# A cross-attention and feed-forward kernel: the scale parameters loaded behind the first token tile, and the hand-written order of five engines rewritten

## The chip, the cores and the metric

One core of one Trainium2 chip runs the kernel. The time is the device time of one execution in microseconds (us), the median over runs. "Words" of 4 bytes are float32; a "tile" of tokens is 128 tokens of 2048 features.

## The reference

Two stages on x of shape (2, 1024, 2048), both with a residual sum:

```python
def fake_quant(x, scale, zp):
    q = jnp.clip(jnp.round(x / scale + zp), 0, 255)
    return (q - zp) * scale
x = x + fake_quant(layernorm(x), s1, z1) @ fake_quant(ctx, s2, z2)   # ctx (2, 2048, 2048)
u = layernorm(x)
probs = softmax(u @ W_router.T); top 2 of 8 experts, renormalised -> w
base = u @ W_base.T + b_base                                          # W_base (2048, 2048)
lora = einsum('ter,eor,te->to', einsum('td,erd->ter', u, lora_A), lora_B, w) * 2.0
x = x + base + lora                                                   # 8 experts of rank 16
```

Both scales are 8/255, both zero points 128. The four numbers arrive as a small input (`qp`), so the kernel reads them at run time.

## The kernel before

Everything is one program for one core, with explicit semaphores. `XA`, `EX`, `Q`, `S` are the large buffers on the chip, `PS` the 8 banks in which TensorE sums, `par`, `cst`, `rr`, `flag`, `WC`, `mv`, `st` small ones.

**The first matmul.** For each of the 16 token tiles: `xn_load` (L375) brings it in two halves, `ln1_stats` (L573, L578) makes mean and variance on VectorE, `ln1_coef` (L583 to L593) makes scale and offset from them and from the parameters in five small steps on GpSimd, `ln1_quant` (L607) quantises to one byte on ScalarE or VectorE, `ln1_turn` (L625) transposes on TensorE, `ln1_back` (L635, L637) brings the result back as bf16. Between the first transposes stand filler matmuls (`warm`, L650), whose result nobody reads. The 32 slices `g` of ctx (16 for each batch) come by `ctx_load` (L380), are quantised by `ctx_quant` (L662 on ScalarE) and turned into bf16 by `ctx_conv` (L672, L674). `gemm1` (L694) multiplies them, a half of 512 tokens and 8 of 16 blocks of the sum at a time, and `evac1` (L706, L709) adds x. `keep` stores the sum to the output in DRAM.

**The second normalisation.** Of batch 0 the sums over features are made along the way: `add0`, `square0`, `sqadd0` add up on GpSimd and ScalarE, `offset_total` (L826) and `var_total` (L839) turn the sums into one number a token by one-column matmuls against `mean_w`, 8 for the offsets and 8 for the variances. `y_scale`, `y_high`, `y_diff1` to `y_diff4` and `y_low` (L1031) make seven operands out of the normalised tokens, each as a float16 value and a float16 remainder. Those of batch 1 are made later, go to DRAM (`yd_store`, 64 pieces) and come back by seven `y_load`s of 2048 KB, one for each operand, when batch 0 is done with the buffers.

**The second matmul.** `lora_h` (L1087 to L1089) gives lora_A times the tokens, `route` (L1163) the router's logits. Then 16 pairs `i` of row blocks of W_base, 8 for each batch, each as seven products (`product`, L1470 to L1472, 24 matmuls each, by which four quarters of a pair come from seven multiplications instead of eight), with tails for the experts (`tail`, L1483 to L1485), `post` (L1526, L1532) for scale and bias, and `store` (L537), by which GpSimd has a DMA add the result onto the output in DRAM. The weights of pair `i` come by `raw_load` in two halves; `w_squares` (L1325), `w_norm` (L1338), `w_total` (L882, one matmul of one column), `w_root` (L886) and `w_factors` make a scale from them, `w_scale` (L1377), `w_add` (L1402, L1406, L1415), `w_high` (L1422) and `w_low` (L1428) their float16 operands.

**What sets the order.** Each engine has its own list of calls, written out by hand: `sync_program`, `tensor_program`, `scalar_program`, `vector_program`, `pool_program`, some 1,900 calls in all. An engine works strictly through its list; each call first waits for its semaphores. Which engine does a call, and the count at which a semaphore stands for it, come from tables (`BACK`, `CTXQ`, `YLO`, `WLO`, `POST`, `WSC`, `KEEP`, `GEMM`, `EVAC`, `WHI`, `PROD`), which have to follow the order of the lists. Ahead of the lists `sync_first`, `vector_first` and `pool_first` run. Then every engine asks in `case_of` (L1999 to L2001) which case the parameters make:

```python
eng.wait_ge(*par_ok["flag"])
return eng.value_load(flag[0:1, 0:1], min_val=0, max_val=2)
```

`params` (L554 to L565) has VectorE make eight small values out of `par`, the last of them `flag` (0 where both zero points are 128). A flag above 0 sends the engines through `general_...` first, which these inputs do not need.

## Time and profile before

| | before |
|---|---|
| median of 3 runs (lowest, highest) | 960.43 us (956.87, 961.31) |
| the profiled execution, its span | 960.41 us, 958.6 us |
| mean granted clock of TensorE, share of full speed | 0.996 |
| TensorE busy, matmul | 931.6 us, 97% |
| TensorE busy, weight load (beside it) | 443.1 us, 46% |
| VectorE, ScalarE, GpSimd busy | 585.5, 506.9, 310.2 us |
| instructions | 13081 |
| read from DRAM, written to it | 137.44 MB, 56.62 MB |

The span runs from the first to the last instruction of the core; the time of the execution has 1.8 us more. A busy time says how long an engine had work under way, not that it was held up by nothing: a matmul at half the clock counts as busy. The loss at half the clock is therefore to be had only from the granted clock of single stretches. PE in the rows is TensorE, DVE VectorE, ACT ScalarE, POOL GpSimd, SP SyncE; a "q" behind the name is that engine's DMA issue. In the column of waits, "a <- b" says that the instruction of line a began when the one of line b was done.

### The profile page before, as it was taken

The page shows a single profiled execution, that of the slowest core. Times are in us where ns is not written, and L with a number is a line of the kernel's source. Part 1 is how long each engine was busy: PE and PEld are TensorE (multiplying, and loading weights), DVE is VectorE, ACT ScalarE, POOL GpSimd, SP SyncE. Part 2 cuts the span into 40 slices and gives each one's busy share as a digit, 9 for nine tenths or more (in the row PEclk, how much of TensorE's full clock was granted, in tenths as well). Part 3 has the DMA queues.
Part 4 walks back from the last instruction along what each step waited for, and adds up shares of the span by engine and source line. Part 5 has one row for each costly group of instructions (what it writes and reads, how often), then busy time and mean ns, then how long its engine had stood idle before and what let it go on. Part 6 is the DMA issues. An engine that isn't in the chain of part 4 may idle for free. (4 is left out here: it accounts for less than half of the span.)

```text
span 958.6 us, 13081 instructions
## 1 busy us (share of the span) xinstructions
PE 931.6 (97%) x4594; PEld 443.1 (46%) x4614; DVE 585.5 (61%) x729; ACT 506.9 (53%) x495; POOL 310.2 (32%) x249
## 2 busy tenths in 40 slices
PE   4899999999999999999999999999999999999998
PEld 3754445444444443444444444444444444444443
DVE  6886877899787846566877977326432524425421
ACT  4866894668864737465575665334422322342320
POOL 4574985273532253261212212150210202111200
PEclk9999999999999999999999999999999999999999
DMA  9999698879835676657678767987314223342331
GB/s 345 412 412 393 219 376 298 299 255 307 293 67 181 198 243 209 221 146 242 200 211 276 181 223 188 345 308 214 117 22 116 50 93 72 98 123 75 85 66 44
DMA packets 61445, 197.08 MB, mean 206 GB/s; under 512 B 5696, under 2 KB 22208, under 8 KB 52928
## 3 DMA queue, kind: packets, MB, share of 16 engines
q1 hardware_dynamic: 55904, 176.26, 50.9%
q0 software_dynamic: 5472, 19.93, 12.6%
q8 instruction: 41, 0.67, 0.3%
q14 instruction: 28, 0.23, 0.1%
HBM read 137.44 MB, written 56.62 MB: 202 GB/s over the span
## 5 line engine op out<-in xcount | busy, mean ns | idle before, releaser
L1470 PE MATMUL PS<-XA,Q 128*128 128x512 f16 x384 | 145.6, 379 | 0.0
L1472 PE MATMUL PS<-XA,Q 128*128 128x512 f16 x384 | 145.5, 379 | 0.0
L1471 PE MATMUL PS<-XA,Q 128*128 128x512 f16 x384 | 145.5, 379 | 0.0
L1428 POOL TENSOR_TENSOR S<-S 128x1024 f16<-128x1024 f32 x29 | 64.6, 2233 | 169.4 <-ACT S L1422 169.4
L694 PE MATMUL PS<-Q,S 128*128 128x512 bf16 x501 | 112.7, 383 | 2.2 <-DVE S L709 1.3
L694 PE MATMUL PS<-EX,S 128*128 128x512 bf16 (+1 forms) x535 | 105.7, 354 | 3.5 <-POOL S L674 1.6
L1422 ACT ACTIVATE Q<-S 128x1024 f16<-128x1024 f32 x64 | 66.6, 1050 | 73.2 <-PE PS L1472 29.5
L1470 PE MATMUL PS<-EX,S 128*128 128x512 f16 x256 | 97.0, 379 | 0.5 <-ACT Q L1532 0.5
L1471 PE MATMUL PS<-EX,S 128*128 128x512 f16 x256 | 97.0, 379 | 0.0
L1472 PE MATMUL PS<-EX,S 128*128 128x512 f16 x256 | 97.0, 379 | 0.0
L1377 ACT ACTIVATE S<-S,WC 128x1024 f32<-128x1024 f32 x64 | 70.7, 1137 | 46.1 <-DMA S<-in_wT_dram 31.4
L1422 ACT ACTIVATE S<-S 128x1024 f16<-128x1024 f32 x48 | 49.6, 1051 | 78.1 <-DVE S L1406 26.1
L1428 DVE TENSOR_TENSOR Q<-S,Q 128x1024 f16<-128x1024 f32 x52 | 64.2, 1244 | 40.5 <-ACT Q L1422 40.5
L1526 DVE SCALAR_TENSOR_TENSOR Q<-PS,WC,Q 128x512 f32<-128x512 f32 x36 | 26.8, 748 | 92.6 <-PE PS L1485 75.8
L694 PEld LDWEIGHTS PS<-Q,S 128*128 128x128 bf16 x512 | 50.3, 99 | 64.3 <-issue 4.4
L694 PEld LDWEIGHTS PS<-EX,S 128*128 128x128 bf16 x544 | 53.0, 98 | 52.4 <-issue 2.4
L662 ACT ACTIVATE S<-S,cst 128x2048 uint8<-128x2048 f32 x28 | 58.2, 2086 | 19.2 <-DMA S<-in_cT_dram 19.0
L537 POOL DMA_DIRECT2D out_dram<-Q x30 | 26.5, 941 | 124.1 <-DVE Q L1534 64.9
L1470 PEld LDWEIGHTS PS<-XA,Q 128*128 128x128 f16 x384 | 37.6, 98 | 45.7 <-issue 1.1
L1472 PEld LDWEIGHTS PS<-XA,Q 128*128 128x128 f16 x384 | 37.6, 98 | 45.3
L1471 PEld LDWEIGHTS PS<-XA,Q 128*128 128x128 f16 x384 | 37.6, 98 | 45.0 <-issue 0.3
L1428 POOL TENSOR_TENSOR Q<-S,Q 128x1024 f16<-128x1024 f32 x12 | 28.6, 2386 | 90.4 <-ACT Q L1422 90.4
(244 smaller groups left out, 1722.7 us busy)
## 6 DMA issues: line engine op xcount, KB each, us to landing
S<-in_cT_dram SPq DMA_DIRECT2D x32, 1024.0 KB, 7.7
S<-in_wT_dram SPq DMA_DIRECT2D x32, 1024.0 KB, 6.1
out_dram<-Q POOLq DMA_DIRECT2D x30, 512.0 KB, 5.6
EX<-in_xn_dram SPq DMA_DIRECT2D x24, 512.0 KB, 7.7
yops_dram<-S SPq DMA_DIRECT2D x48, 256.0 KB, 3.4
XA<-in_xT_dram SPq DMA_DIRECT2D x16, 512.0 KB, 7.9
out_dram<-XA SPq DMA_DIRECT2D x16, 512.0 KB, 7.6
out_dram<-S SPq DMA_DIRECT2D x16, 512.0 KB, 4.3
```

The costliest lines, as they stand in the source:

```text
L537: e.dma_start(outT[b, o], ob[(2 * i + h) % 3], accum_op=ALU.add).then_inc(stored.of(2 * i + h), 16)
L662: e.activation(u8b[g % 2], ctx_f[g % 2], ACT.Identity, bias=z2, scale=inv2).then_inc(ctxq.of(g), 1)
L694: last = e.matmul(bank(a)[:, t0 % 512:t0 % 512 + t1 - t0], q2[q][:, 128 * k:128 * (k + 1)], q1T[b][:, k, t0:t1], start=(k == 0), stop=(k = ...
L1377: e.activation(v, v, ACT.Copy, bias=0.0, scale=w_cols(i)[:, 4:5]).then_inc(w_scaled.of(i, q), 1)
L1422: e.activation(ring[slot_of(i, n)][:, 0:1024], W_SRC[n], ACT.Copy, bias=0.0, scale=1.0).then_inc(w_hi.of(i, n), 1)
L1428: e.tensor_tensor(v[:, 1024:2048], W_SRC[n], v[:, 0:1024], ALU.subtract).then_inc(w_lo.of(i, n), 1)
L1470: e.matmul(bank(bk), wh, yh(op, k), start=(fresh and k == 0), stop=False, skip_group_check=not fresh)
L1471: e.matmul(bank(bk), wh, yl(op, k), start=False, stop=False, skip_group_check=not fresh)
L1472: last = e.matmul(bank(bk), wl, yh(op, k), start=False, stop=(read and k == 7), skip_group_check=not fresh)
L1526: e.scalar_tensor_tensor(dst, src, kk, dst, op0=ALU.mult, op1=ALU.add).then_inc(post_ok.of(i, n), 1)
```

## The change

`load_par` goes from the head of SyncE's list to behind the first token tile's `xn_load`, and VectorE makes the first tile's statistics ahead of `params`. The lists of all five engines are rewritten. No call changes its engine and none is added or removed; the tables are reordered to follow. Two lines of them and the pieces of the lists of which the text speaks:

```diff
@@ -49,68 +49,68 @@
     ('sq', 1), ('sq', 3)]}
...
     def sync_first(e):
-        load_par(e); xn_load(e, 0, 0); xn_load(e, 0, 1); xn_load(e, 0, 2); ctx_load(e, 0); xn_load(e, 0, 3); ctx_load(e, 1)
+        xn_load(e, 0, 0); load_par(e); xn_load(e, 0, 1); xn_load(e, 0, 2); ctx_load(e, 0); xn_load(e, 0, 3); ctx_load(e, 1)
...
-        x_load(e, 17, general); keep(e, 12); keep(e, 16); ctx_load(e, 21); load_bias(e); ctx_load(e, 20)
...
-        x_load(e, 24, general); b_load(e, 0); keep(e, 23); ctx_load(e, 28); x_load(e, 25, general); keep(e, 24)
...
+        x_load(e, 24, general); ctx_load(e, 28); keep(e, 23); x_load(e, 25, general); keep(e, 24); ctx_load(e, 29)
...
-        ln_load(e, 7); yd_store(e, 7, 0); yd_store(e, 7, 4); raw_load(e, 8, 1); yd_store(e, 7, 3); yd_store(e, 7, 2)
-        yd_store(e, 7, 6); yd_store(e, 7, 1); yd_store(e, 7, 7); yd_store(e, 7, 5); a_reload(e); b_load(e, 8); y_load(e, 0)
-        raw_load(e, 8, 0); y_load(e, 1); y_load(e, 2); y_load(e, 3); y_load(e, 5); y_load(e, 4); raw_load(e, 9, 1)
...
+        keep(e, 30); keep(e, 31); tile_load(e, 0); tile_load(e, 1); load_bias(e); raw_load(e, 1, 1); b_load(e, 1)
...
+        yd_store(e, 6, 6); ln_load(e, 7); raw_load(e, 8, 1); a_reload(e); yd_store(e, 7, 3); yd_store(e, 7, 2)
+        yd_store(e, 7, 6); yd_store(e, 7, 1); yd_store(e, 7, 5); yd_store(e, 7, 0); yd_store(e, 7, 7); yd_store(e, 7, 4)
+        raw_load(e, 8, 0); y_load(e, 0); y_load(e, 1); y_load(e, 2); y_load(e, 3); y_load(e, 5); y_load(e, 4); b_load(e, 8)
...
     def tensor_program(e):
...
-        gemm1(e, 18, 0, 512, 0, 8); gemm1(e, 18, 512, 1024, 0, 8); offset_total(e, 0); offset_total(e, 1)
-        var_total(e, 0, 0); var_total(e, 0, 1); gemm1(e, 18, 0, 512, 8, 16); gemm1(e, 18, 512, 1024, 8, 16)
...
+        r_total(e); gemm1(e, 17, 0, 512, 8, 16); offset_total(e, 0); offset_total(e, 1); gemm1(e, 18, 0, 512, 0, 8)
+        gemm1(e, 18, 0, 512, 8, 16); var_total(e, 0, 0); gemm1(e, 19, 512, 1024, 0, 8); var_total(e, 0, 1)
...
-        gemm1(e, 31, 0, 512, 8, 16); lora_h(e, 0, [0]); w_total(e, 0); lora_h(e, 0, [1]); lora_h(e, 0, [2])
-        lora_h(e, 0, [3]); lora_h(e, 0, [4]); lora_h(e, 0, [5]); lora_h(e, 0, [6]); lora_h(e, 0, [7])
...
+        gemm1(e, 31, 512, 1024, 8, 16); lora_h(e, 0, [0]); w_total(e, 0); lora_h(e, 0, [1]); lora_h(e, 0, [2])
+        lora_h(e, 0, [3]); lora_h(e, 0, [4]); lora_h(e, 0, [5]); lora_h(e, 0, [6]); clear(e, 0); lora_h(e, 0, [7])
-        product(e, 0, 0, 4, 5); clear(e, 0); product(e, 0, 0, 5, 6); product(e, 0, 0, 6, 7); product(e, 0, 0, 7, 8)
...
-        product(e, 1, 2); product(e, 1, 3); product(e, 1, 4); tail(e, 1, 2); w_total(e, 2); product(e, 1, 5)
...
+        product(e, 1, 3); product(e, 1, 4); w_total(e, 2); tail(e, 1, 2); product(e, 1, 5); product(e, 1, 6); tail(e, 1, 0)
...
-        ctx_quant(e, 19); square0(e, 14); square0(e, 15); ctx_quant(e, 18); add1_first(e); ctx_conv(e, 18); ctx_quant(e, 20)
...
-        copy(e, 7); y_high(e, 1, 7, "B"); y_high(e, 1, 7, "A"); y_high(e, 1, 7, "T"); y_high(e, 1, 7, "4"); w_scale(e, 8, 3)
-        w_high(e, 7, 5); post(e, 7, 2); a_high(e, 1, 0); a_high(e, 1, 1); w_scale(e, 8, 2); w_scale(e, 8, 0)
...
+        ctx_quant(e, 19); ctx_quant(e, 18); square0(e, 15); ctx_conv(e, 18); add1_first(e); ctx_quant(e, 21)
...
+        w_high(e, 7, 4); post(e, 6, 6); y_high(e, 1, 7, "T"); w_high(e, 7, 5); y_high(e, 1, 7, "4"); b_high(e, 7)
+        post(e, 7, 2); w_scale(e, 8, 3); w_scale(e, 8, 2); a_high(e, 1, 0); a_high(e, 1, 1); w_high(e, 8, 1); post(e, 7, 3)
...
     def vector_first(e):
-        params(e)
+        ln1_stats(e, 0, 0); params(e)
...
-        w_low(e, 1, 5); store(e, 0, 0); w_low(e, 1, 6); sqadd1(e, 6); sqadd1(e, 8); w_root(e, 2); store(e, 0, 1)
-        w_low(e, 2, 2); store(e, 1, 0); w_low(e, 2, 6); sqadd1(e, 9); w_low(e, 2, 5); sqadd1(e, 10); w_root(e, 3)
...
+        sqsum1_move(e, 1); sqadd1(e, 2); sqsum1_move(e, 3); w_low(e, 1, 2); sqadd1(e, 4); store(e, 0, 0); store(e, 0, 1)
+        w_low(e, 1, 5); w_low(e, 1, 6); sqadd1(e, 6); sqadd1(e, 8); w_root(e, 2); w_low(e, 2, 2); store(e, 1, 0)
```

The instructions of SyncE's queue at the start, before (`in_qp` holds the parameters, `in_xn` the token tiles, `in_cT` the slices of ctx; the first two tiles lie in `EX`):

```order
L362 DMA par<-in_qp_dram 128x4
L375 DMA EX<-in_xn_dram 128x1024 x4
L375 DMA XA<-in_xn_dram 128x1024 x2
L380 DMA S<-in_cT_dram 128x2048
L375 DMA XA<-in_xn_dram 128x1024 x2
```

And now:

```order
L375 DMA EX<-in_xn_dram 128x1024 x2
L362 DMA par<-in_qp_dram 128x4
L375 DMA EX<-in_xn_dram 128x1024 x2
L375 DMA XA<-in_xn_dram 128x1024 x2
L380 DMA S<-in_cT_dram 128x2048
```

The parameters have moved behind the two halves of the first tile. On VectorE the first tile's statistics (L573, L578) have moved ahead of the small values (L556 and on), in the same way:

```order
 L2028 UNCONDITIONAL_BRANCH
+L573 BN_STATS st<-EX 128x6 x4
+L578 BN_AGGR mv<-st 128x2
 L556 RECIPROCAL cst<-par 128x1
 L557 RECIPROCAL cst<-par 128x1
```

TensorE in the first matmul, where the sums of batch 0 become one number a token (L826 the offsets, L839 the variances, L694 the first matmul, about 165 us into the program):

```order
+L694 MATMUL PS<-Q,S 128x512 x8
 L826 MATMUL PS<-mean_w,S 128x1 x8
-L839 MATMUL PS<-mean_w,S 128x1 x8
-L694 MATMUL PS<-Q,S 128x512 x80
+L694 MATMUL PS<-Q,S 128x512 x16
+L839 MATMUL PS<-mean_w,S 128x1 x4
+L694 MATMUL PS<-Q,S 128x512 x8
+L839 MATMUL PS<-mean_w,S 128x1 x4
+L694 MATMUL PS<-Q,S 128x512 x72
```

The variances' eight one-column matmuls stood right behind the offsets'; now 16 matmuls of `gemm1` stand between, and 8 more between the halves.

GpSimd around the first stores of the second matmul (L537 `store`, L1428 `w_low`, L819 `sqadd1`, L886 `w_root` of pair 2):

```order
+L1428 TENSOR_TENSOR Q<-S,Q 128x1024
 L819 TENSOR_TENSOR S<-S 128x1024
-L1428 TENSOR_TENSOR Q<-S,Q 128x1024
-L1428 TENSOR_TENSOR S<-S 128x1024
-L537 DMA out_dram<-Q 128x1024
-L1428 TENSOR_TENSOR S<-S 128x1024
+L537 DMA out_dram<-Q 128x1024 x2
+L1428 TENSOR_TENSOR S<-S 128x1024 x2
 L819 TENSOR_TENSOR S<-S 128x1024 x2
 L886 TENSOR_TENSOR WC<-WC,cst 128x1
```

The first store has moved ahead of one `w_low`, and the second from behind `w_root` to right behind the first.

## Rows read from the trace of the kernel before

**Rows 1.** Of the page, part 1: busy us and share of the span, instructions.
```profile
PE 931.6 (97%) x4594; PEld 443.1 (46%) x4614; DVE 585.5 (61%) x729; ACT 506.9 (53%) x495; POOL 310.2 (32%) x249
```

**Rows 2.** Waits of TensorE: what, line <- releaser: us, times, longest us.
```profile
PE PS L625 <- ACT S L607: 13.6, 2, 12.3
PE PS L882 <- DVE WC L1338: 2.1, 1, 2.1
...
PE PS L694 <- DVE S L709: 1.3, 2, 1.1
PE PS L1087 <- DVE XA L1031: 1.0, 1, 1.0
PE PS L1470 <- ACT Q L1532: 0.5, 1, 0.5
...
PE PS L694 <- ACT S L672: 0.3, 1, 0.3
```

**Rows 3.** Busy by stretch: us, PE, PEld, DVE, ACT, POOL; PEclk, DMA, GB/s.
```profile
165.00:167.70 2.70, 2.62 (x23) 2.47 (x24) 2.70 (x4) 0.33 (x1) 0.00 (x0) 1.00 0.97 252
167.70:171.20 3.50, 3.50 (x10) 1.29 (x9) 2.66 (x5) 3.50 (x2) 0.00 (x0) 0.51 1.03 419
365.70:369.20 3.50, 3.50 (x10) 1.20 (x9) 2.58 (x7) 2.57 (x3) 1.31 (x2) 0.51 0.53 60
```

**Rows 4.** Timeline of SyncE's queue at the start: start us, us, what.
```profile
0.74 0.39 SPq L362 DMA_DIRECT2D par<-in_qp_dram  x1
1.18 1.84 SPq L375 DMA_DIRECT2D EX<-in_xn_dram  x4
```

**Rows 5.** DMA issues: KB each, us from issue to landing.
```profile
Braw<-in_rT_dram SPq DMA_DIRECT2D x1, 64.0 KB, 9.5
par<-in_qp_dram SPq DMA_DIRECT2D x1, 2.0 KB, 1.6
```

**Rows 6.** Timeline of VectorE from 2.4 us.
```profile
2.40 0.16 DVE L556 RECIPROCAL cst<-par 128x1 f32<-128x1 f32 x1 [2.40 <-DMA par<-in_qp_dram]
3.09 0.16 DVE L565 TENSOR_TENSOR flag<-rr 128x1 int32<-128x1 f32 x1
5.50 2.56 DVE L573 BATCH_NORM_STATS2 st<-EX 128x6 f32<-128x512 f32 x4 [2.25 <-DMA EX<-in_xn_dram]
8.10 0.26 DVE L578 BATCH_NORM_AGGREGATE mv<-st 128x2 f32<-128x24 f32 x1
```

**Rows 7.** Timeline of ScalarE from 4.5 us.
```profile
4.48 1.28 ACT L607 ACT_TABLE_LOAD   x1 [4.48 <-issue]
...
10.18 2.09 ACT L607 ACTIVATE S<-EX,mv 128x2048 uint8<-128x2048 f32 x1 [4.42 <-POOL mv L593]
16.32 2.09 ACT L662 ACTIVATE S<-S,cst 128x2048 uint8<-128x2048 f32 x1 [0.96 <-DMA S<-in_cT_dram]
23.33 2.10 ACT L607 ACTIVATE S<-XA,mv 128x2048 uint8<-128x2048 f32 x1 [1.17 <-POOL mv L593]
```

**Rows 8.** Timeline of TensorE at the second transpose.
```profile
13.24 4.05 PE L650 MATMUL PS<-mean_w 128*128 128x128 bf16 x36
```

**Rows 9.** Timeline of ScalarE around the conversion of ctx 27.
```profile
223.48 2.09 ACT L662 ACTIVATE S<-S,cst 128x2048 uint8<-128x2048 f32 x1 [3.08 <-DMA S<-in_cT_dram]
...
228.50 1.91 ACT L672 ACTIVATE S<-S 128x2048 bf16<-128x2048 uint8 x1
```

**Rows 10.** Timeline of GpSimd and ScalarE around the first store.
```profile
348.68 0.87 POOL L537 DMA_DIRECT2D out_dram<-Q  x1
...
359.48 0.78 ACT L1532 ACTIVATE Q<-PS,bo,WC 128x512 f32<-128x512 f32 x1 [1.99 <-DMA out_dram<-Q]
```

**Rows 11.** The chain that ended last, at 588 us.
```profile
588.69 7.57 DMA S<-in_wT_dram
```

**Rows 12.** Timeline of VectorE at the last operands of lora_A.
```profile
606.14 2.48 DVE L1068 SCALAR_TENSOR_TENSOR Q<-S,cst,Q 128x1024 f16<-128x1024 f32 x2 [0.17 <-ACT Q L1056]
```

**Rows 13.** The stretch behind 616 us, columns as in rows 3.
```profile
616.00:620.00 4.00, 4.00 (x20) 1.86 (x19) 0.00 (x0) 3.89 (x5) 1.92 (x1) 1.00 1.05 388
```

607 lines of the change are left out of this document (304 added, 303 removed), and 80 rows, old and new, of tables (EVAC, GEMM, POST, PROD).

## The prediction, on record before the changed kernel ran

> **What bounds the kernel now.** I read the page's busy times first, then TensorE's waits, its granted clock by stretches, and the timelines around each wait. TensorE is busy 931.6 us of a span of 958.6 [rows 1], so a gain can only come from its start, its waits and its clock. Its waits by cause [rows 2] add up to little behind the start: 13.6 us for the first tiles' transposes, then single waits of 2.1, 1.1, 1.0, 0.5 and 0.3 us. The clock adds a loss that no wait shows: from 167.7 to 171.2 us it was granted at 0.51, the 1.2 GHz level, where it stood at 1.00 before [rows 3], and a second such stretch of the same length and level begins at 365.7, in the same rows. Each costs 3.5 x (1 - 0.51) = 1.7 us. Everything else on VectorE, ScalarE, GpSimd and the queues lies beside TensorE's work. What can be had is therefore the start plus 5.0 us of waits plus 3.4 us of clock. The profiled execution took 960.41 us and the median of the three runs is 960.43, so the sum below stands against either.
>
> **The first tile.** SyncE now issues the parameters ahead of the tile [rows 4]. In the new order the tile's first half leaves 0.44 us earlier (1.18 less 0.74), so the statistics start at 5.50 - 0.44 = 5.06 and the moments end at 8.10 + 0.26 - 0.44 = 7.92 [rows 6]. The parameters leave third, at about 0.74 + 2 x 0.44 = 1.6. Alone they landed 1.6 us after issue; a small load into the full queue took 9.5 us [rows 5]. The four statistics ran without a gap, so the tile's second half had landed by 6.8; I take the parameters to land right behind it, nearest to the row of the empty queue, hence before 7.92.
>
> The price of the move is another one. Every engine reads a flag that the last of the small operations writes, and only then enters its program. That flag is ready at 3.09 + 0.16 = 3.25 now [rows 6], long before anybody needs it. Behind the moments it is ready at 7.92 + 0.85 = 8.77, with 0.85 us for the small operations as now (2.40 to 3.25). ScalarE's table load begins 4.48 - 3.25 = 1.23 us after the flag [rows 7], so engines open at about 10.0. GpSimd's five coefficient steps stand behind that gate; the first quantisation starts 10.18 - 8.36 = 1.8 us after the moments today, so now at 10.0 + 1.7 = 11.7: **1.5 us later, not earlier**. ScalarE has idled 0.96 us before 16.32 and 1.17 us before 23.33 [rows 7], 2.1 us together. The 36 filler matmuls behind the first transpose, 4.05 us [rows 8], shift with it and hold the second transpose back by about another 1.1, still ahead of the fourth tile's quantisation at 23.33. I carry +0.1; bounds are -0.4 (the earlier issue reaches all tiles, the gate hides) and +1.5 (nothing is absorbed). SyncE reads the flag later too, but its next load waits for that first quantisation anyway, and the queue still holds loads then: 0.
>
> **The re-order, by the waits it touches.**
> - ctx_conv(18) stood behind add1_first on ScalarE and now stands ahead of it: the 0.3 us wait [rows 2] goes, -0.3.
> - The moment sums of the first batch are one-column matmuls in a row, offsets and variances; the clock fell right behind them, with TensorE busy 2.62 of the last 2.70 us [rows 3]. Now gemm pieces stand between them, in groups of 8. I take the fall away: -1.7, bounds 0 and -1.7. The Trainium skill's page "TensorE: Matmul & The Clock Gate", section "HAM oscillation — how this bites in real kernels", puts falls down to idle gaps. No idle gap stood before this one, so the trace differs; by the page's rule splitting the sums would change nothing, and the sum would be 1.7 us higher.
> - At 229.5 us TensorE waits 1.1 us before gemm1(27, 0). The list puts it down to evac1 [rows 2], but the half that ended last is not one that this piece needs; it needs ctx_conv(27), which ended at 228.50 + 1.91 = 230.41 [rows 9] and is late because ScalarE sat 3.08 us for ctx 28 [rows 9]. ctx_load(28) stood behind keep(23); now it goes ahead of it, about 1.1 us earlier, when ctx_quant(26) has ended. The 1.1 us wait goes: -1.1, bounds 0 and -1.3.
> - At 284 us TensorE waits 1.0 us for y_low(0,7,A) [rows 2]. clear(0) now stands ahead of the last lora_h piece and needs the next VectorE operation too: +0.6, bounds 0 and +1.2.
> - w_total(2) waits 2.1 us [rows 2]. ScalarE was held 1.99 us before post(1,1) by store(0,0), which GpSimd issued at 348.68 behind w_low(1,5) [rows 10]; w_squares(2) is queued behind. Now the two stores go ahead of that w_low, some 2.1 us earlier, while the raw halves that w_squares(2) also needs come 0.9 us later for the second store's issue. I take -1.9 and, with the wait, the second fall of the clock, -1.7; bounds 0 and -3.8.
> - At 599 us TensorE waits 0.5 for post(7,2). The chain behind it is a weight load of 7.57 us [rows 11], for which w_scale(8,3) sat ahead of w_high(7,5) and post(7,2) on ScalarE; both are now ahead of it: -0.5.
> - The bias load goes from the middle of the first matmul to behind the first tile loads; its readers come some 20 us later: 0.
> - Engine assignments and instruction counts stay; arithmetic costs nothing new.
>
> Sum: 0.1 - 0.3 - 1.7 - 1.1 + 0.6 - 1.9 - 1.7 - 0.5 = -6.5, that is 953.9. But hundreds of positions change, and I followed only those where a wait stands today. A rewritten order brings waits of its own; its bounds are nothing, and all that is removed. Between them I take half, +3.2: **957.1 us**. The nearest evidence is the kernel itself, whose order shows five waits behind its start.
>
> **The rivals.**
> 1. *No new waits.* All gains stand: 953.9. For it: none of the waits of rows 2 lies behind 600 us today, a third of the span.
> 2. *Waits only change places.* 960.4, 959.5 to 961.5. For it: rows 2 show short waits spread over several causes, as any order close to its limit has. Here the table does not do what it seems to.
> 3. *The gate reaches TensorE.* If the parameters land 9.5 us after issue [rows 5], at 11.1, the flag comes at about 12.0 and the first quantisation at 14.9, 4.7 us later. Less the idle time of 1.2 us left before 23.33, 3.5 us pass on: 957.1 + 3.4 = 960.5. If they are early but the slack is not there, 957.1 + 1.4 = 958.5. The Trainium skill's page "DMA: Bandwidth & Descriptors", section "Queues, rings and completion order", says that an engine consumes descriptors in ring order; by it only the tile's two halves stand ahead, which speaks for the early landing. The unhindered second half agrees.
> 4. *The operand loads of the second batch, on the slower side.* raw_load(8,0), which waits for a_low(1,1), now stands ahead of y_load(0) on SyncE; it stood behind it. a_low(1,1) ends at 606.14 + 2.48 = 608.62 today [rows 12]; from 616 us on the queues move 388 GB/s at a full share [rows 13]. If it still ends then, y_load(0)'s 128 x 8 x 512 words of 4 bytes, 2.1 MB, are added to that traffic: 2.1 / 0.388 = 5.4 us, for lora_h(1) and all behind it. Each us that a_low(1,1) ends earlier takes one off. Since w_high(7,5) and a_reload come earlier, I expect about 605.3, and up to 2.1 us of wait, which lies in the +3.2. But raw_load(8,1) now waits for w_low(7,4), which has moved behind w_add(7,5), and both a_high stand behind it on ScalarE: if a_low(1,1) ends at 610, the wait is 6.8 and the time 957.1 + 6.8 = 963.9. It decides the sign from an end of 606.5 on, where the wait is 3.3.
>
> **How the numbers follow.** Chances: the forecast 0.37, rival 1 0.23, rival 2 0.18, rival 3 0.12, rival 4 0.10. A measurement of this kernel can tell about 0.5%, 4.8 us, from no change: below 955.6 is faster, above 965.2 slower. Faster gets rival 1 and a fifth of the forecast, 0.30. Slower gets the half of rival 4 in which a_low(1,1) ends behind 611.3 (957.1 + 8.1 = 965.2), and a wait that I did not see, 0.08. The rest, 0.62, is no change that can be told. The range is 953.0 to 963.0: it takes in the forecast, rivals 2 and 3 whole, most of rival 1 and the lower part of rival 4.
>
> **What would show it.** In the changed kernel's trace: the flag at about 8.8 and the first quantisation near 11.7 on ScalarE, yet the fourth tile's near 23.4; TensorE's clock at 1.00 near 165 us and near 365; no wait for ctx_conv(27) above 0.3 us; w_total(2) waiting under 0.5; the waits of lora_h(1) for yops loads at most 2 us. Wrong it would be if the quantisation of the fourth tile came later than 24, if the clock fell again although the sums are split, or if waits that no row shows today add up to more than 6.5 us.

## The result: 26 us slower

| | before | changed |
|---|---|---|
| median of 6 runs (lowest, highest) | 960.5 us (956.87, 961.31) | 986.46 us (980.15, 989.47) |
| ratio, 95% interval | 1 | 1.0271 [1.024, 1.0302] |
| profiled execution, its span | 960.41, 958.6 us | 987.43, 985.6 us |

The prediction was 957.1 us, with a range of 953 to 963. It was wrong in its sign. The page's busy times of the changed kernel, to be held against [rows 1]:

```profile
PE 931.8 (95%) x4593; PEld 440.8 (45%) x4614; DVE 602.9 (61%) x729; ACT 508.0 (52%) x495; POOL 311.7 (32%) x249
```

TensorE does the same work in the same busy time, so the whole loss is time in which it waits. (Either execution has about 3 us of its busy time from half the clock: before in two stretches of 3.4 us, now in one of 6.8.) VectorE works 17.4 us longer with the same 729 instructions.

I cut the program at two points that both kernels have, the first `lora_h` matmul of each batch. **Start** is all ahead of the first transpose, **stage A** runs from there to the first `lora_h` of batch 0, **stage B** to the first `lora_h` of batch 1, **stage C** to the last matmul. TensorE by these stretches, before and then changed (columns: stretch, length, busy (instructions), granted clock, DMA share, GB/s):

```profile
0.00:12.33 12.33, 0.00 (x0) 1.00 0.82 280
12.33:265.54 253.21, 246.22 (x1289) 0.99 0.89 328
265.54:617.32 351.78, 347.39 (x1676) 1.00 0.69 207
617.32:954.26 336.94, 336.94 (x1630) 1.00 0.40 111
```

```profile
0.00:15.38 15.38, 0.01 (x1) 1.00 0.86 314
15.38:275.80 260.42, 244.60 (x1288) 1.00 0.86 314
275.80:634.91 359.11, 346.28 (x1676) 1.00 0.66 201
634.91:981.27 346.36, 339.89 (x1630) 0.99 0.38 110
```

Length less busy is idle time. Before it is 12.3, 7.0, 4.4 and 0.0 us; changed it is 15.4, 15.8, 12.8 and 6.5. All four stretches lose: 3.1, 7.2, 7.3 and 9.4 us, together 27.0, which is the difference of the two profiled executions. Of the 9.4, 6.5 are idle and 2.9 are a longer busy time, from a stretch at half the clock. TensorE's waits of the changed kernel, against [rows 2]:

```profile
PE PS L625 <- issue: 15.4, 1, 15.4
PE PS L694 <- DVE S L709: 6.3, 4, 2.9
PE PS L1087 <- DMA XA<-yops_dram: 6.0, 1, 6.0
PE PS L882 <- DVE WC L1338: 4.1, 3, 2.1
PE PS L1470 <- issue: 2.8, 1, 2.8
PE PS L1470 <- ACT Q L1532: 2.2, 1, 2.2
PE PS L739 <- DVE S L868: 1.8, 1, 1.8
PE PS L1470 <- ACT PS L1504: 1.8, 2, 1.3
```

Before, that list was short behind its first line. Now it holds three sizes: one of 15.4 at the start, one of 6.0 for a load, and many of 1 to 3 us. The experiments take them one by one.

**The start.** The first steps of the changed kernel, from the timeline, against [rows 4, 6, 7]:

```profile
0.74 0.87 SPq L375 DMA_DIRECT2D EX<-in_xn_dram  x2
...
1.65 0.43 SPq L362 DMA_DIRECT2D par<-in_qp_dram  x1
...
8.29 0.16 DVE L565 TENSOR_TENSOR flag<-rr 128x1 int32<-128x1 f32 x1
...
11.62 2.09 ACT L607 ACTIVATE S<-EX,mv 128x2048 uint8<-128x2048 f32 x1 [0.64 <-POOL mv L593]
...
15.38 1.09 PE L625 MATMUL PS<-ident,S 128*128 128x128 f32 x4 [15.38 <-issue]
```

Flag and quantisation come within 0.4 us of the prediction (8.8, 11.7). But the quantised tile is there at 13.71, and TensorE starts at 15.38, with no releaser named. What it does until then is the branch of `case_of` past the general case, for which the trace has a record on TensorE's weight-load queue. Before, and then changed (duration in ns three times, start in us twice):

```profile
L2017 PEldq COMPARE_BRANCH  x1: 6671/6671/6671, 4.1 to 4.1; - x1
```

```profile
L2017 PEldq COMPARE_BRANCH  x1: 5850/5850/5850, 9.4 to 9.4; - x1
```

TensorE needs 6 to 7 us for that one branch. On the other four engines the same branch has 45 to 50 ns. ScalarE's first instruction came 1.23 us after the flag [rows 7], and I had taken that for every engine. Before, the branch ended at 4.1 + 6.7 = 10.8, and the quantised tile, there only at 12.3, hid it. Now it ends at 9.4 + 5.9 = 15.2 and nothing does. The other runs bear this out: the record is there in all eighteen profiled executions, with 5.85 to 6.67 us, and in the ten in which TensorE's first matmul has no releaser it starts 0.16 or 0.17 us behind the record's end.

**The batch switch.** TensorE waits at 645 for the first operand of batch 1, and the clock stands at half behind it. Five-us stretches of the changed kernel (busy times of PE, PEld, DVE, ACT, POOL, then clock, DMA share, GB/s):

```profile
630.00:635.00 5.00, 5.00 (x25) 2.29 (x24) 4.20 (x3) 4.56 (x6) 3.39 (x3) 1.00 1.05 389
635.00:640.00 5.00, 5.00 (x25) 2.26 (x24) 0.00 (x0) 1.60 (x2) 5.00 (x4) 1.00 1.07 334
640.00:645.00 5.00, 5.00 (x25) 2.25 (x23) 1.23 (x1) 0.00 (x0) 2.82 (x2) 1.00 1.07 251
645.00:650.00 5.00, 0.43 (x2) 0.00 (x0) 0.00 (x0) 0.00 (x0) 0.00 (x0) 1.00 1.03 306
650.00:655.00 5.00, 3.55 (x9) 1.35 (x10) 0.00 (x0) 0.00 (x0) 0.00 (x0) 0.50 1.06 396
```

The DMA engines are at a full share throughout, yet the rate falls from 389 to 251 GB/s in the middle. Before, it held 388 over [rows 13], and 385 and 387 in the two stretches behind 625:

```profile
625.00:630.00 5.00, 5.00 (x25) 2.25 (x23) 0.00 (x0) 3.11 (x4) 4.10 (x2) 1.00 1.05 385
630.00:635.00 5.00, 5.00 (x24) 2.25 (x23) 1.23 (x1) 0.00 (x0) 2.20 (x2) 1.00 1.05 387
```

GpSimd's timeline of the changed kernel says what came in between:

```profile
633.71 0.87 POOL L537 DMA_DIRECT2D out_dram<-Q  x1
...
636.79 0.87 POOL L537 DMA_DIRECT2D out_dram<-Q  x1
...
639.47 1.19 POOL L537 DMA_DIRECT2D out_dram<-Q  x1
```

These are three of the stores that add onto the output in DRAM. Before, they went out together behind the loads, at 642.95, which is 25.6 us behind the first `lora_h` of batch 1; now the first goes out 1.2 us ahead of it.

A second thing has moved. `y_load(0)`, the first of the operand loads, went out 16.5 us ahead of that `lora_h` before (600.80 for 617.32) and goes out 11.1 us ahead of it now (623.86 for 634.91).

**The middle.** Two lines of VectorE's and one of GpSimd's timeline in stage B of the changed kernel:

```profile
401.07 5.19 DVE L819 TENSOR_TENSOR S<-S 128x1024 f32<-128x1024 f32 x1 [4.08 <-ACT S L814]
...
408.58 1.23 DVE L819 TENSOR_TENSOR S<-S 128x1024 f32<-128x1024 f32 x1
```

```profile
400.67 4.51 POOL L1428 TENSOR_TENSOR S<-S 128x1024 f16<-128x1024 f32 x2
```

The same addition takes 5.19 us while GpSimd has two `w_low` in a row, and 1.22 or 1.23 us the four other times. Taking every VectorE operation that is over 0.5 us above the median of its own line and shape, the excess adds up to 17.3 us before and 34.5 changed; in stage B 10.1 and 24.9. The Trainium skill, page "SBUF — State Buffer", section "Who interferes with whom", says that a VectorE instruction with two inputs in SBUF contends with a GpSimd instruction that reads SBUF. The rows agree: GpSimd's two are done at 400.67 + 4.51 = 405.18, and the addition ends at 406.26, about its own duration behind them.

### The profile page after: what moved, and what is told of

Read it like the earlier page. It is cut to its first block and busy times, and to the rows that moved or that the text cites. A ratio compares the mean times of both kernels' runs of the same rounds, so it can differ in the third digit from the quotient of the medians.

```text
span 985.6 us, 13080 instructions
## 1 busy us (share of the span) xinstructions
PE 931.8 (95%) x4593; PEld 440.8 (45%) x4614; DVE 602.9 (61%) x729; ACT 508.0 (52%) x495; POOL 311.7 (32%) x249
## 3 DMA queue, kind: packets, MB, share of 16 engines
q0 software_dynamic: 5472, 19.93, 11.7%
## 5 line engine op out<-in xcount | busy, mean ns | idle before, releaser
L1428 POOL TENSOR_TENSOR S<-S 128x1024 f16<-128x1024 f32 x29 | 67.9, 2353 | 207.7 <-ACT S L1422 207.7
L694 PE MATMUL PS<-Q,S 128*128 128x512 bf16 x500 | 111.6, 379 | 7.8 <-DVE S L709 6.3
L694 PE MATMUL PS<-EX,S 128*128 128x512 bf16 (+1 forms) x535 | 106.3, 354 | 5.1 <-POOL S L674 1.6
L1428 DVE TENSOR_TENSOR Q<-S,Q 128x1024 f16<-128x1024 f32 x52 | 71.8, 1383 | 40.1 <-ACT Q L1422 40.1
L694 PEld LDWEIGHTS PS<-Q,S 128*128 128x128 bf16 x512 | 49.7, 99 | 68.0 <-issue 8.2
L694 PEld LDWEIGHTS PS<-EX,S 128*128 128x128 bf16 x544 | 52.7, 98 | 55.2 <-issue 4.2
L537 POOL DMA_DIRECT2D out_dram<-Q x30 | 26.8, 931 | 129.6 <-issue 57.0
L1428 POOL TENSOR_TENSOR Q<-S,Q 128x1024 f16<-128x1024 f32 x12 | 27.5, 2293 | 73.7 <-ACT Q L1422 73.7
```

The lines of the kernel that those rows point to most:

```text
L537: e.dma_start(outT[b, o], ob[(2 * i + h) % 3], accum_op=ALU.add).then_inc(stored.of(2 * i + h), 16)
L694: last = e.matmul(bank(a)[:, t0 % 512:t0 % 512 + t1 - t0], q2[q][:, 128 * k:128 * (k + 1)], q1T[b][:, k, t0:t1], start=(k == 0), stop=(k = ...
L1428: e.tensor_tensor(v[:, 1024:2048], W_SRC[n], v[:, 0:1024], ALU.subtract).then_inc(w_lo.of(i, n), 1)
```

## The experiments

Each group (e, f, g, h) ran beside the kernel before on one chip, on three different chips in all; the medians of the kernel before were 959.74, 959.22, 960.54 and 960.66 us for the four groups. The stages come from each one's profiled execution, cut as above.

| kernel | median (range), runs | ratio [95%] | start | A | B | C |
|---|---|---|---|---|---|---|
| before | 960.5 | 1 | 12.3 | 253.2 | 351.8 | 336.9 |
| changed | 986.46 | 1.0271 | 15.4 | 260.4 | 359.1 | 346.4 |
| e1_gate_alone | 961.21 (959.05–966.5), 10 | 1.0019 [0.9993, 1.0045] | 15.5 | 252.0 | 348.4 | 336.9 |
| e2_after_old_start | 989.14 (984.62–990.96), 4 | 1.0288 [1.0227, 1.0349] | 12.5 | 261.9 | 362.0 | 345.1 |
| e3_old_until_lora | 977.97 (977.79–978.63), 4 | 1.0178 [1.0127, 1.0229] | 12.4 | 249.7 | 362.5 | 347.1 |
| e4_new_until_lora | 967.26 (964.3–969.67), 10 | 1.0073 [1.0038, 1.0109] | 15.5 | 258.4 | 350.3 | 336.9 |
| f1_new_from_pair7 | 967.78 (961.7–972.03), 10 | 1.009 [1.006, 1.0119] | 12.4 | 250.7 | 348.0 | 346.2 |
| f2_operand_loads | 985.05 (978.32–987.72), 4 | 1.0257 [1.0196, 1.0319] | 15.7 | 254.5 | 361.7 | 345.6 |
| f3_old_queue_first | 984.48 (984.19–988.31), 4 | 1.0272 [1.0227, 1.0318] | 15.7 | 257.8 | 358.0 | 347.1 |
| f4_old_vector_middle | 1008.86 (1006.09–1012.99), 4 | 1.0525 [1.0473, 1.0577] | 15.3 | 259.4 | 380.2 | 346.3 |
| g1_stores_later | 983.29 (976.57–986.58), 4 | 1.0252 [1.0216, 1.0288] | 15.6 | 254.4 | 362.4 | 338.0 |
| g2_loads_and_stores | 979.55 (977.3–982.73), 4 | 1.0197 [1.0158, 1.0236] | 15.8 | 260.0 | 362.8 | 336.9 |
| g3_port | 986.91 (984.66–988.55), 4 | 1.0272 [1.0236, 1.0308] | 15.6 | 259.0 | 362.1 | 345.2 |
| g4_three_repairs | 964.88 (962.28–967.25), 9 | 1.0054 [1.0031, 1.0077] | 14.9 | 252.4 | 352.6 | 336.9 |
| h1_urgent_first | 988.05 (984.35–994.15), 4 | 1.027 [1.0201, 1.0339] | 15.9 | 263.7 | 359.5 | 346.5 |
| h2_and_stores | 972.74 (971.38–975.37), 4 | 1.0119 [1.0071, 1.0167] | 12.4 | 257.4 | 359.1 | 337.7 |
| h3_and_first_stage | 981.25 (978.78–986.25), 4 | 1.0208 [1.015, 1.0266] | 12.5 | 265.4 | 361.0 | 337.3 |
| h4_before_stores_early | 958.65 (956.59–961.74), 10 | 0.9985 [0.996, 1.001] | 12.3 | 253.3 | 350.1 | 336.9 |

Read down the columns. C has two values, near 337 and near 346. B has two, 348 to 353 and 358 to 363, and one far out. A varies most: the ten executions whose lists agree with the changed kernel's over stage A read from 254.4 (g1) to 263.7 (h1), the five with the old lists from 249.7 to 253.3. So two single readings of A that differ by less than 9 us say nothing.

### One: the start

`e1_gate_alone` is the kernel before with only the two changes of the start; `e2_after_old_start` undoes them in the changed one.

```diff
-load_par(e); xn_load(e, 0, 0)        # sync_first
+xn_load(e, 0, 0); load_par(e)
-params(e)                            # vector_first
+ln1_stats(e, 0, 0); params(e)
```

> The kernel before with only its start changed: parameters behind the first token tile on SyncE, the first tile's statistics ahead of the small values on VectorE. Theory A (the loss is spread: the start costs its own part, and each rewritten stage its own): the first transpose about 3 us later than before, near 15.4, and by the fifth tile 1.7 us are left; the time is 960.5 + 1.7 = 962.2. Theory B (the later start shifts every engine against the queues, and the waits behind it come from that): over 970. Rival: the start is absorbed wholly, 960.5.

> The changed kernel with the old start: parameters first, the small values ahead of the statistics. Theory A: 986.5 - 1.7 = 984.8, the first transpose back at about 12.3. Theory B: most of the 26 us goes, under 972.

Alone, the first transpose comes 3.2 us later (15.5), and the time moves by +1.5 us with an interval that holds zero. Part of the delay is taken up behind it, as in the changed kernel: from the fourth tile on, each quantisation is 1.8 us later than before (1.66 in the changed kernel). Removed from the changed kernel, the start is back at 12.5, and the total shows no gain: four runs with a spread of 6 us can't show 1.7 us. The start is the smallest of the terms, and its two changes are not what costs 26 us.

### Two: which stage's lists cost what

The lists were cut at matching calls and spliced. `e3_old_until_lora` has the old lists up to about the first `lora_h` and the old start, then the new ones; `e4_new_until_lora` the reverse; `f1_new_from_pair7` has the new lists only from the start of pair 7 on, which is 39 us ahead of the `lora_h` of batch 1. The edit in short form, the same for each engine's list:

```diff
-order = before[:first_lora_h] + before[first_lora_h:]
+order = before[:first_lora_h] + after[first_lora_h:]     # e3
+order = after[:first_lora_h] + before[first_lora_h:]     # e4
+order = before[:pair_7] + after[pair_7:]                 # f1
```

> Every engine's list as before up to about the first lora_h, as in the changed kernel behind it. In the changed trace the first lora_h stands 10.3 us later than before, the end 27.0 us. Theory A (each stage bears the waits its own order makes): 960.5 + 27 - 10.3 = 977. Theory B (lateness handed on from the first stage makes the later waits): 960.5 to 964.

> The complement: lists of the changed kernel up to about the first lora_h, as before behind it. Theory A: 960.5 + 10.3 = 970.8. Theory B: near 986. If the two halves together give clearly more or less than 27 us, they are not independent.

> Every engine's list as before up to the start of pair 7 (SyncE up to the last load for the operands of batch 1), as in the changed kernel behind it. In the changed trace the first lora_h of batch 1 stands 17.6 us later than before and the end 27.0, so 9.4 us are lost behind it, in one wait of 6.0 us for an operand load and TensorE at half clock right behind that wait. If this loss is made by the order in this place alone: 960.5 + 9.4 = 970, with that wait and the half clock in the trace. If it needs the lateness of the stages before: 960.5 to 963.

Against the kernel before beside them: e3 +18.2 (interval 12.2 to 22.0), e4 +7.5 (3.6 to 10.5), f1 +8.6 us (5.8 to 11.4). The first two add up to 25.7 of the 26.0: within these intervals the halves don't act on each other, and a loss that needs both is excluded. From e3 and f1, stage B alone costs 18.2 - 8.6 = 9.6, and from e4 and e1 stage A costs 7.5 - 1.5 = 6.0. The account of the medians: **start 1.5, A 6.0, B 9.6, C 8.6**. As differences, A is known by it to about 4 us and B to about 6. The stage table gives a second reading: the means of the executions whose lists agree differ by 7.1 us in A (ten new, five old) and by 11.1 in B (seven new, four old). f1 also says that C's loss needs nothing new ahead of pair 7: its waits have the 6.0 us for the load, as in the changed kernel.

```profile
PE PS L1087 <- DMA XA<-yops_dram: 6.0, 1, 6.0
```

### Three: stage C, by two theories

The prediction's rival 4 put the danger at this very place and named SyncE's order: `raw_load(8, 0)` ahead of `y_load(0)`. `f2_operand_loads` restores that order.

```diff
-raw_load(e, 8, 1); a_reload(e); yd_store(e, 7, ...)  x8; raw_load(e, 8, 0); y_load(e, 0)
+yd_store(e, 7, ...)  x4; raw_load(e, 8, 1); yd_store; a_reload(e); yd_store  x3; y_load(e, 0); raw_load(e, 8, 0)
```

> The changed kernel with ten calls of SyncE re-ordered: the stores of the last operands of batch 1 in the order in which they become ready, raw_load(8,1) and a_reload between them instead of ahead of them, y_load(0) ahead of raw_load(8,0). If what makes the 9.4 us is that loads with a late release stand ahead of stores and loads that are ready: y_load(0) goes out near 617 instead of 623.9, the fourth operand lands before it is needed, the wait and the half clock go, 986.5 - 9.4 = 977. Rival: the queue's bandwidth sets it, the wait only shrinks by a us or two, 984 or more.

`y_load(0)` went out 5.9 us earlier by the clock (617.98 for 623.86), but 2.9 of these only because `lora_h` came earlier too: its lead is 14.0 us, for 11.1 in the changed kernel and 16.5 before. C stayed at 345.6. The wait is still there, in two parts, and so is the fall of the rate:

```profile
PE PS L1087 <- DMA XA<-yops_dram: 5.6, 2, 2.9
```

```profile
635.00:640.00 5.00, 5.00 (x25) 2.29 (x24) 0.00 (x0) 1.56 (x2) 5.00 (x4) 1.00 1.06 332
640.00:645.00 5.00, 2.46 (x12) 0.90 (x10) 1.23 (x1) 0.00 (x0) 2.76 (x2) 1.00 1.08 250
645.00:650.00 5.00, 4.59 (x22) 2.15 (x23) 0.00 (x0) 0.00 (x0) 0.00 (x0) 1.00 1.03 313
```

So half of the lost lead, given back, took 0.4 us off the wait. `g1_stores_later` leaves SyncE alone and puts the three stores back behind `w_low(8, 6)`; `g2_loads_and_stores` does both.

```diff
 w_low(e, 8, 0)
-store(e, 7, 0)
 w_low(e, 8, 2)
-store(e, 6, 1)
 w_low(e, 8, 4)
-store(e, 7, 1)
 w_low(e, 8, 3); w_low(e, 8, 5); w_low(e, 8, 6)
+store(e, 7, 1); store(e, 6, 1); store(e, 7, 0)
```

> The changed kernel with three of GpSimd's accumulating stores, (7,1), (6,1) and (7,0), behind the last w_low of pair 8, as before; SyncE's list unchanged. In the changed trace they are issued at 633.7, 636.8 and 639.5, and the transfers fall from 389 GB/s to 334, 251 and 306 in the 15 us behind 635; before they stood at 643 and the rate stayed at 385 to 387. If these stores take the bandwidth from the operand loads: (3 x 387 - 334 - 251 - 306) x 5 us = 1.35 MB more in that time, 3.5 us, so the wait of 6.0 falls to about 2.5 and the time to 980 to 983. If the late start of the loads is all: wait unchanged at 6, 986.

> Both edits of this place: SyncE's ten calls as in f2_operand_loads and GpSimd's three stores behind pair 8's w_low. f2 left 2.9 and 2.6 us of wait for operand loads. With 3.5 us of bandwidth back the first goes to 0 and the second under 1, and no half clock follows: 986.5 - 6 - 3.4 = 977. If the place has another limit, waits of over 3 us stay and the time is over 982.

In g1 the wait for the load is gone from the list (I had expected 2.5 us to be left), the clock shows no stretch at half behind it, and C is 338.0, with `y_load(0)` no further ahead than in the changed kernel (11.1 us). Its windows:

```profile
635.00:640.00 5.00, 5.00 (x25) 2.29 (x24) 1.23 (x1) 0.00 (x0) 3.50 (x2) 1.00 1.06 387
640.00:645.00 5.00, 5.00 (x25) 2.29 (x24) 0.00 (x0) 0.00 (x0) 0.00 (x0) 1.00 1.05 382
645.00:650.00 5.00, 5.00 (x25) 2.27 (x24) 0.00 (x0) 0.00 (x0) 0.00 (x0) 1.00 1.05 387
```

That settles stage C in the profiles: 8.4 of its 9.4 us are the three stores among the loads, and with the load order as well (g2) it is 336.94, as before. The eight executions with the stores at -1, 2 and 5 us from that `lora_h` have C from 345.1 to 347.1; the four with the stores 26 us and more behind it (g1, g2, h2, h3) have 336.9 to 338.0, three of them with the short lead of 11 us. The stores' 3 x 512 KB are little against the 14 MB of operands, but the rate of all traffic falls by a third while they run. The medians of few runs don't show it as well: g1's is only 3.2 us below the changed kernel's, with four runs spread over 10 us, of which the profiled one is the fastest (976.57), and g2's is 6.9 below. For the size, f1's +8.6 from ten runs is the better evidence.

`h4_before_stores_early` was to show the same from the other side, in the kernel before, with the three stores ahead of `w_low(8, 6)`.

> The kernel before with the stores (7,0), (6,1) and (7,1) ahead of w_low(8,6) on GpSimd, so that they go out near 631 instead of 643, while the operand loads are under way. In the kernel before the fourth operand landed 1.2 us before it was needed. If stores take 3.5 us from the loads: a wait of 1 to 2.5 us for an operand load, with the segment behind lora_h of batch 1 at 338 to 343 instead of 336.9, and 962 to 966. If they do not: 336.9 and 960.5.

```profile
640.42 2.67 POOL L537 DMA_DIRECT2D out_dram<-Q  x3 [10.81 <-DVE Q L1526]
```

It tested nothing: the first store still waited for `post` on VectorE and went out at 640.42, when the operand loads were through. Moving a call in a list does not move it in time when its own input is later. The time was the same, 0.9985. So the stores' effect is shown by taking them away, in four kernels, and not by putting them in.

### Four: stages A and B, where the theories fell

`f3_old_queue_first` gives the changed kernel SyncE's old list in stage A; `f4_old_vector_middle` VectorE's old list between the first `lora_h` and pair 7. In short form:

```diff
-sync = after[:first_lora_h] + after[first_lora_h:]
+sync = before[:first_lora_h] + after[first_lora_h:]      # f3
-vector = ... + after[first_lora_h:pair_7] + ...
+vector = ... + before[first_lora_h:pair_7] + ...        # f4
```

> The changed kernel with SyncE's list as before in the first matmul's stage (up to about 310 us), all other engines as changed. If the order of loads and stores makes the 6 us that this stage loses beside the start: 980.5. If the other engines' lists make them: 986 or more, since loads then fit the consumers less well.

> The changed kernel with VectorE's list as before between the first lora_h and pair 7, all other engines as changed. If the 7.3 us that this stretch loses come from VectorE's order: 979. If from no single engine's list: 984 to 990.

f3 stays at 984.5, between its two expectations and 2 us below the changed kernel, with the intervals overlapping. f4 is 22 us **slower** still, above both of its expectations, with B at 380 and TensorE's waits in it at 25 us for 13. One engine's old list among four new ones fits them worse than its new one. A swap of one engine's list therefore doesn't tell whose order is bad, and this holds for f3 too: it doesn't clear SyncE's order in A.

The profiles say more of where the two stages lose than any of these swaps. TensorE's waits over 0.2 us add up, in stage A, to 4.8 to 5.7 us in the six executions with old lists and to 7.7 to 16.3 in the twelve with new ones; in stage B to 2.7 to 5.3 in the six with old lists (f1's up to pair 7) and, f4 aside, to 10.0 to 13.7 in the others. And in stage B they come back at the same places. In the eight executions with the changed kernel's lists there (changed, e2, e3, f2, f3, g1, g2, and g3 with its one edit):

| wait of TensorE | us behind the first `lora_h` | in how many of 8 | us |
|---|---|---|---|
| `w_total(1)` | 47 | 8 | 1.2 to 2.5 |
| `w_total(2)` | 99 | 8 | 1.1 to 2.8 |
| a product, for `copy` (L1504) | 125 | 7 | 1.0 to 2.3 |
| a product, for `post` (L1532) | 139 | 8 | 2.2 to 3.4 |
| a product, for `w_low` (L1428) | 252 | 8 | 1.0 to 1.2 |
| a product, no releaser named | 283 | 7 | 1.3 to 3.2 |

With the old lists only `w_total(2)` of these waits. In stage A one wait of 1.3 to 1.9 us, of `spread` for `var_diag` (L739 for L868), is in eleven of the twelve and in none of the six.

`g3_port` takes the held addition of stage B apart, by putting GpSimd's `w_low`s between its two `sqadd1`:

```diff
 store(e, 1, 0)
+w_low(e, 2, 6)
 sqadd1(e, 9)
+w_low(e, 2, 5)
 sqadd1(e, 10)
 store(e, 1, 1)
-w_low(e, 2, 6)
-w_low(e, 2, 5)
```

> The changed kernel with seven calls of GpSimd in the order of before: w_low(2,6) and w_low(2,5) between the sqadd1 of 9 and 10 instead of behind them. In the changed trace VectorE's sqadd1(11), 1.2 us elsewhere, takes 5.19 us from 401.07, until GpSimd's w_low(2,6) and w_low(2,5) have ended at 405.17; ScalarE's post(2,2) stands behind, and TensorE waits 2.2 us at 410.6. If a VectorE operation with two inputs on the chip is held by GpSimd's: sqadd1(11) back to under 2.6 us and the 2.2 us wait gone, 984. If it was late for another reason, its time and the wait stay.

```profile
407.20 1.23 DVE L819 TENSOR_TENSOR S<-S 128x1024 f32<-128x1024 f32 x1 [10.51 <-POOL S L819]
```

The addition is back at 1.23 us, and starts 6 us later, since it now waits for `sqadd1(10)`: it ends at 408.43, for 406.26 in the changed kernel. A hold became a dependency at least as long. TensorE's wait there, which I had expected to go, is 3.4 us for 2.2, and the time did not move (986.91). The 17 us of VectorE's extra busy time are real, but at this spot removing them was worth nothing.

`h1_urgent_first` takes the largest single waits of stage B and moves what TensorE waits for ahead of what held it: `post(1, 4)` ahead of `centre1(9)`, `w_add(5, 2)` and `w_low(6, 0)` ahead of parts of `y_low` and `y_scale` on VectorE, `post(2, 2)` ahead of `square1(13)` on ScalarE, and `w_total(1)`, `w_total(2)` later on TensorE. `h2_and_stores` adds the stores' old place and the old start. `h3_and_first_stage` adds six such moves in stage A.

```diff
-centre1(e, 9); post(e, 1, 4)                                      # vector, h1
+post(e, 1, 4); centre1(e, 9)
-y_low(e, 1, 3, "T"); y_low(e, 1, 3, "4"); w_add(e, 5, 2)          # vector, h1
+w_add(e, 5, 2); y_low(e, 1, 3, "T"); y_low(e, 1, 3, "4")
-square1(e, 13); post(e, 2, 2)                                     # scalar, h1
+post(e, 2, 2); square1(e, 13)
...
-ctx_conv(e, 23); evac1(e, 21, 1)                                  # vector, h3
+evac1(e, 21, 1); ctx_conv(e, 23)
-ctx_quant(e, 31); ctx_conv(e, 30)                                 # scalar, h3
+ctx_conv(e, 30); ctx_quant(e, 31)
```

> The changed kernel with six calls of the middle moved, each one that TensorE waits for and that stood behind a call which itself waits: post(1,4) ahead of centre1(9), w_add(5,2) ahead of y_low(1,3,T) and w_low(6,0) ahead of y_scale(1,5,B) on VectorE, post(2,2) ahead of square1(13) on ScalarE, w_total(1) four pieces and w_total(2) one tail later on TensorE. In the changed trace the waits at these places are 1.5, 1.0, 2.8, 2.2, 2.2 and 1.2 us, 10.9 together. Theory (the order makes each): from the first lora_h to that of batch 1 the changed kernel takes 359.1, before 351.8; now 350 to 353, time 976 to 979. Rival (the engines behind are late anyway, the waits move to the next call): over 357, time 984 or more.

> h1 with the three stores of GpSimd behind pair 8's w_low and the old start as well. From the first lora_h of batch 1 to the last matmul 337 to 338 instead of 346.4; first transpose at 12.4. By theory: 986.5 - 9 (stores) - 1.5 (start) - 8 = 968. By the rival: 976.

> h2 with six calls of the first stage moved in the same way: ctx_conv(10) ahead of ln1_stats(1,6), evac1(10,1) ahead of ln1_stats(1,7), evac1(21,1) ahead of ctx_conv(23), both evac1 of 22 ahead of y_low(0,1,B) on VectorE, ctx_conv(30) ahead of ctx_quant(31) on ScalarE. From the first transpose to the first lora_h the changed lists took 254 to 262 in eight runs, the old ones 250 to 253 in five. Theory: 252 to 255, time 962 to 966. Rival: 257 or more, no faster than h2.

h1's stage B is 359.5, the changed kernel's 359.1: nothing gained by six moves, each at a place with a wait of 1 to 3 us. TensorE's list in h1 shows why:

```profile
PE PS L1470 <- ACT PS L1504: 6.7, 3, 3.4
PE PS L1087 <- DMA XA<-yops_dram: 6.4, 1, 6.4
PE PS L694 <- DVE S L709: 4.8, 4, 2.0
```

The waits for `copy` (L1504) were 1.8 us in the changed kernel and are 6.7 here; the waits at 139 and 283 are gone or down to 0.4, `w_total(1)`'s has passed to a product 3 us behind it (2.1). h3, which was to gain, came out 8.5 us above h2; its A read 265.4 for 257.4, which by itself is within what equal lists differ by. In h1 moving a call ahead helped its reader and delayed others. h2 is 15.3 us below h1. The stage table has 3.5 of it at the start and 8.8 in C, from its two edits; stage A, which they hardly touch, read 6.3 lower in that one execution. It is the best version of the new lists, between its two expectations, and still 12 us above the kernel before.

### Five: the repairs that the prediction counted

`g4_three_repairs` is the kernel before with three pieces of the change: the earlier load of the first tile, and the two edits on which the gains of -1.1 and -1.9 rested.

```diff
-load_par(e); xn_load(e, 0, 0)                        # sync_first
+xn_load(e, 0, 0); load_par(e)
-keep(e, 23); ctx_load(e, 28)                         # sync
+ctx_load(e, 28); keep(e, 23)
-w_low(e, 1, 5); store(e, 0, 0); ...; store(e, 0, 1)  # pool
+store(e, 0, 0); store(e, 0, 1); w_low(e, 1, 5); ...
```

> The kernel before with three pieces of the change alone: the tile's first load ahead of the parameters (VectorE still makes the small values first), ctx_load(28) ahead of keep(23), store(0,0) and store(0,1) ahead of w_low(1,5). By the terms of the prediction: -0.5, -1.1, -1.9, so 957.0, without a wait of w_total(2) and before gemm1(27,0). Rival, waits only change places: 960 to 962.

Its median is 4.3 us higher (interval 3.0 to 7.4), above both expectations. Its span is 961.2 us for 958.6, which is as much as its first transpose is later (14.92 for 12.33). The edits of `ctx_load(28)` and of the stores brought nothing, A 252.4 and B 352.6. Both waits that they were to remove stand at the same matmuls, and both are longer, 2.4 for 1.1 and 2.5 for 2.1:

```profile
PE PS L882 <- DVE WC L1338: 2.5, 1, 2.5
PE PS L694 <- DVE S L709: 2.4, 1, 2.4
```

The second line is the wait ahead of the first matmul of slice 27 (231.06 us), the first line `w_total(2)` (366.89 us). The one at slice 27 shows a misreading. In the kernel before, the piece that waits is `gemm1(27, 512, 1024, 0, 8)`, the second half of the tokens, and its call waits for `evac1(25, 1)`. That is the later of the two `evac1` here. Before, and then in g4:

```profile
229.77 0.74 DVE L709 SCALAR_TENSOR_TENSOR S<-PS,cst,S 128x512 f32<-128x512 f32 x1
230.66 1.67 PE L694 MATMUL PS<-Q,S 128*128 128x512 bf16 x7 [1.11 <-DVE S L709]
```

```profile
227.58 1.91 ACT L672 ACTIVATE S<-S 128x2048 bf16<-128x2048 uint8 x1
...
230.17 0.74 DVE L709 SCALAR_TENSOR_TENSOR S<-PS,cst,S 128x512 f32<-128x512 f32 x1
```

Before, `evac1(25, 1)` ended at 230.51, 0.1 us behind `ctx_conv(27)` (230.41), and TensorE went on 0.15 us later. In g4 the conversion is 0.9 us earlier (229.49), and TensorE again goes on 0.15 us behind `evac1`, which ended at 230.91. The wait list had named the right releaser.

The wait of `w_total(2)` is one that single executions give very differently. Over the executions with the old lists in stage B, `w_total(2)` waits 2.1, 0.4, 1.1, 0.2, less than 0.2 and 2.5 us (before, e1, e4, f1, h4, g4). In e1 and f1 ScalarE was held by `store(0, 0)` for 0.4 us and not for 1.99. In g4 the two stores go out at 347.57 and ScalarE isn't held by them at all, and the wait is the longest of the six.

No version that was run beats the kernel before by more than its interval.

## Why the prediction was wrong

- **The step that failed** is "A rewritten order brings waits of its own; its bounds are nothing, and all that is removed. Between them I take half, +3.2". The measured +26.0, less the sum's -6.5 and the 1.4 by which the start came out above its term, leaves 31 us for that step's 3.2, if the sum's gains are taken as they stand; if they brought nothing, as g4 has it for two of them, it is 26.0 - 1.5 = 24.5. The upper bound had no ground: nothing ties what a new order costs to what the old one lost. The evidence named for it, five short waits, describes an order that fits. f4 shows how far an order that doesn't fit goes: +22 us from one list of one engine in one stage.
- **The start.** Taken +0.1, bounds up to +1.5; e1 gives +1.5 (interval -0.7 to +4.3), and the first transpose is 3.05 later. The gate was seen, and its price for ScalarE was right to 0.1 us. It failed at "ScalarE's table load begins 4.48 - 3.25 = 1.23 us after the flag [rows 7], so engines open at about 10.0": TensorE opens 6.9 us after the flag. [Rows 8] show TensorE only from 13.24 on, and I didn't ask since when it could have. The sign named for it came: the fourth tile's quantisation began at 24.99, 1.66 later than before, and not near 23.4.
- **Landing of the parameters.** Taken as right behind the tile's second half, hence before 7.92. In the changed kernel the first value is made of them at 7.67; in g4, where VectorE makes them first, they had landed by 6.31, which is 4.7 us after issue. Right, and rival 3's 9.5 us were not reached.
- **ctx_load(28), -1.1.** The reading was wrong: `evac1(25, 1)` ended last, as g4 shows. In the changed kernel no wait stands ahead of slice 27, but waits of 1.1, 0.9 and 2.9 us stand ahead of slices 26, 28 and 30; with the same lists, g1 and g2 have 0.9 and 1.8 us ahead of slice 27 again.
- **The stores of pair 0, -1.9.** In the changed kernel w_total(2) still waits 1.1 us and w_total(1), which moved four pieces ahead, 2.1. The 2.1 us to be removed were those of one execution; the same lists also gave 0.2.
- **The clock, -3.4.** Neither the fall at 167 nor that at 365 is in the changed kernel, as forecast. For the second the reason given fits: before, it began 0.8 us behind the wait of w_total(2). Nearly all others begin so too. From 30 us on and ahead of the batch switch the eighteen profiled executions have 34 stretches at 1.2 GHz, none to four in each. 31 of them begin during a wait of 1.9 to 4.4 us or within 1.6 us behind it, where the engine had been at 2.4 GHz; of the 56 waits of that size, about half have one. The three others are the fall at the one-column sums, in the kernel before, e1 (170.7) and h4 (168.1), with no wait over 0.2 us in the 7 us ahead of it. It is missing in e3, f1 and g4, which have the old sums too, and in all twelve with the split ones. So the split may have won its 1.7 us in those executions that would have lost them; no run changes the sums alone. What the term left out is that every new wait of 2 us can bring such a stretch with it. The Trainium skill's page "TensorE: Matmul & The Clock Gate", section "HAM oscillation — how this bites in real kernels", puts falls down to idle gaps. The prediction had held that one fall against it; the 31 agree with it in kind.
- **clear(0), +0.6; ctx_conv(18), -0.3; post(7, 2), -0.5.** All are below what stage A or B vary by. In the changed kernel's profile none of the three places has a wait over 0.2 us; what that is worth in total, nothing here measures.
- **Rival 4** had the place (the operand loads at the batch switch) and the size ("the wait is 6.8"; 6.0 measured). It had the wrong cause. Its own mechanism did occur, `y_load(0)` lost 5.5 us of its lead, but g1, with that lead still lost, has no wait for a load, and f2, with half of it back, has 5.6 us. a_low(1, 1) ended at 621.68, outside the 605 to 610 considered, but 13.2 us ahead of its `lora_h`, for 8.7 before. What the rival left out was GpSimd's queue. The three stores were in the diff of `pool_program`, and the rate on which the rival rested (388 GB/s, [rows 13]) was measured with no such store in flight. It also left out the clock: half speed for 6.8 us from 650.0 on, which made TensorE's busy time 2.9 us longer. That its figure is near the measured one is luck.
- **The sum as a whole** was built from places where a wait stood before, in one execution. The losses of A, B and C came, but for `w_total(2)`, at places where none stood.

What stays open: which of the several hundred moved calls cost stages A and B their 6.0 and 9.6 us. The splices show that the lists of these stages do it, and the profiles that in B the loss stands in some six waits that come back in execution after execution. Whose order makes them is not shown: f3 and f4 can't tell, and g3 and h1 show only that freeing one held addition, or moving six calls, passes the waits on. That the loss lies in how the five lists fit is the reading that is left, and it is argued, not shown.

## What to carry to other kernels

Where an order written by hand has few waits left, don't price a rewrite by "the waits it removes": here each list fitted the others, and moving calls one by one mostly moved the waits. Read a short wait in several executions before counting on it; the same lists gave 0.2 and 2.1 us at one place. When the wait list names a releaser, look up which piece waits and what its call needs before putting another in its place. Follow each DMA queue separately through a change, GpSimd's stores too, and ask of each load burst whose end somebody waits for what else now runs in it. Before a gate is put later, look up for each engine what it does between the gate and its first instruction, not only for the one that shows it.
